# Three changes together in a fused attention and MLP kernel: a reordered prologue, a product copy moved from VectorE to ScalarE, and one partial sum moved to TensorE

## The reference

```
ada = silu(c) @ Wada.T + bada          # six vectors per batch: shift, scale, gate, twice
h = rmsnorm(x) * (1 + scale_msa) + shift_msa
q, k, v = split_heads(h @ Wqkv.T + bqkv)
q, k = rmsnorm(q) * hd**-0.5, rmsnorm(k)
o = softmax(q @ k.T) @ v
x = x + gate_msa * (o @ Wproj.T + bproj)
h = rmsnorm(x) * (1 + scale_mlp) + shift_mlp
x = x + gate_mlp * (gelu(h @ Wfc1.T + bfc1) @ Wfc2.T + bfc2)
```

## Time and profile before

| | us |
|---|---|
| median of 3 runs | 1811.17 |
| lowest, highest | 1810.55, 1813.67 |
| the profiled execution's own time | 1810.62 |
| its span in the trace | 1808.8 |
| L = 0 begins (first `qk`) | 68.8 |
| L = 64 begins | 343.8 |
| L = 208 begins | 848.2 |
| the MLP's first loop begins, about | 1000 |

### The profile page before, as it was taken

One profiled execution on the slowest core, in us unless ns is written; L12 is line 12 of the kernel. 1 busy time (PEld: TensorE's weight loads), 2 busy tenths in 40 slices (PEclk: granted clock), 3 DMA queues, 4 the chain that ended last, 5 costly groups with the idle time before them and its releaser, 6 DMA issues.

```text
span 1808.8 us, 23247 instructions
## 1 busy us (share of the span) xinstructions
PE 1727.9 (96%) x8376; PEld 1154.5 (64%) x8376; DVE 1085.6 (60%) x1325; ACT 919.6 (51%) x1136; POOL 372.5 (21%) x305
## 2 busy tenths in 40 slices
PE   6998999999999999999889999999999999999998
PEld 3554555555555555554224787878788887878786
DVE  6678888898898898878788545142332324142301
ACT  4476666777777777778787432222221212221221
POOL 3001111100001000000140233333332333333332
PEclk8999999999999999999999899999999999999999
DMA  5754545555555555555765201010020202010000
GB/s 195 214 144 132 135 123 139 132 147 135 154 135 134 146 130 156 127 135 153 174 144 196 74 18 58 25 52 24 12 70 6 64 17 64 17 52 23 17 18 24
DMA packets 122242, 176.92 MB, mean 98 GB/s; under 512 B 29568, under 2 KB 43904, under 8 KB 121136
## 3 DMA queue, kind: packets, MB, share of 16 engines
q1 hardware_dynamic: 115952, 156.41, 32.3%
q10 hardware_dynamic: 5408, 16.81, 2.5%
q0 software_dynamic: 800, 2.62, 0.5%
HBM read 124.87 MB, written 50.92 MB: 97 GB/s over the span
## 4 chain that ended last, share of the span: by engine, by line
PE 44%; issue 29%; DVE 11%; POOL 9%; ACT 4%; DMA 2%; SPq 0%; POOLq 0%; ACTq 0%; DVEq 0%
PE scores L513 9%; PE pv L530 8%; PE gemm L588 7%; DVE sums L791 5%; PE scores L1303 5%; POOL act_parts L1235 5%; PE gemm L601 4%; ACT probs L704 3%; PE pv L1320 3%; PE gemm L1320 2%; PE aux L554 2%; POOL y L1233 2%; PE aux L547 1%; DVE raw L816 1%; DVE raw L862 1%
## 5 line engine op out<-in xcount | busy, mean ns | idle before, releaser
L704 ACT ACTIVATE probs<-scores,shift 128x1024 f32<-128x1024 f32 x512 | 548.7, 1113 | 195.4 <-PE scores L513 178.7
L791 DVE TENSOR_TENSOR sums<-sums,probs 128x2048 f32<-128x2048 f32 x192 | 453.8, 2363 | 32.7 <-ACT probs L704 28.0
L513 PE MATMUL scores<-q_stack,k_stack 128*128 128x512 f32 x1024 | 358.8, 435 | 6.3 <-ACT probs L704 6.1
L1303 PE MATMUL scores<-w_hi,act_parts 128*128 128x512 f32 x1024 | 318.7, 392 | 0.0
L513 PEld LDWEIGHTS scores<-q_stack,k_stack 128*128 128x128 f32 x1024 | 173.8, 189 | 202.3 <-issue 105.5
L1235 POOL TENSOR_TENSOR act_parts<-act_full,act_parts 128x512 fp32r<-128x512 f32 x128 | 172.5, 1348 | 514.2 <-ACT act_parts L1166 513.6
L530 PE MATMUL pv<-probs,v 128*32 128x512 f32 x2048 | 253.1, 603 | 0.4 <-ACT probs L704 0.4
L1303 PEld LDWEIGHTS scores<-w_hi,act_parts 128*128 128x128 f32 x1024 | 191.4, 189 | 38.8
L1303 PE MATMUL scores<-w_lo,act_parts 128*128 128x512 f32 x512 | 199.9, 391 | 0.0
L1373 DVE TENSOR_TENSOR y_next<-pv,p_bias 128x512 f32<-128x512 f32 x28 | 19.3, 691 | 299.7 <-PE pv L1275 299.7
L1166 ACT ACTIVATE act_parts<-act_full 128x512 fp32r<-128x512 f32 x128 | 80.9, 632 | 224.5 <-PE scores L1303 223.5
(11 more groups left out here) (167 smaller groups left out, 1944.1 us busy)
## 6 DMA issues: line engine op xcount, KB each, us to landing
k_stack<-parts_scratch SPq DMA_DIRECT2D x128, 256.0 KB, 5.0
q_stack<-parts_scratch SPq DMA_DIRECT2D x128, 256.0 KB, 5.1
parts_scratch<-parts SPq DMA_DIRECT2D x62, 512.0 KB, 2.9
inverse<-inverse_scratch SPq DMA_DIRECT2D x128, 64.0 KB, 2.1
heads_out<-o_out SPq DMA_DIRECT2D x32, 256.0 KB, 5.2
out<-result SPq DMA_DIRECT2D x32, 256.0 KB, 2.0
heads<-heads_out SPq DMA_DIRECT2D x28, 256.0 KB, 3.6
x_tile<-in_x SPq DMA_DIRECT2D x28, 256.0 KB, 2.8
```

Source lines behind the costliest of these rows:

```text
L513: mm = nc.tensor.matmul(scores[p][:, i, :], k_stack[s][:, h, j * P:(j + 1) * P], q_stack[half][:, h, :], start=True, stop=True)
L704: nc.scalar.activation(probs[L % RING][:, 2 * p:2 * p + 2, :], scores[p][:], ACT.Exp, bias=small["shift"][:]).then_inc(exp_done, 1)
L791: nc.vector.tensor_tensor(sums[:], a[:], probs[l % RING][:], ALU.add).then_inc(added, 1)
L1303: mm = nc.tensor.matmul(acc[t], act_parts[m % 2][:, b, t * P:(t + 1) * P], w2[a][:, m, :], start=(m == 0 and i == 0), stop=(m == NM - 1 an ...
```

## The change

It has three parts, made together.

1. **Prologue.** The first products are now nine, in the order v, k, q, v, v, v, v, k, q; the sixth v tile moves behind L = 0, and the three v tiles of steps 0 to 2 take one step each. The tables of statistics, turns and weight splits are shifted. The four later blocks of `wadaT` are loaded by SyncE as soon as the third block of `wqkvT` has landed, ahead of `v_bias` and `qk_bias` in SyncE's order, in place of ScalarE's queue at L = -14.
2. **Units.** For L >= 0 `raw_out` runs on ScalarE, in the unit's last step behind the step's two exponentials, and `square` follows it at once; the sum of squares comes a step earlier. A third buffer for `raw` is taken from the x tiles, which go from three buffers to two. For batches 2 and 3 the turn of an x tile is a step later (odd steps in place of even ones). `make_parts` always follows the addition of its step in the main loop.
3. **Row sums.** For groups hh >= LEAN = 26 the eighth key tile isn't added by VectorE: TensorE adds it by four more matmuls with `ones` onto the row sums.

```diff
 NU = 2 * NH
 SEEN = HG * CH // P
 XS = 3
+XB = 2
 AFTER = B * BSTEPS
...
@@ -80,11 +81,10 @@
...
-START, AFTER_LAST = -25, 2
-PLAN = placed(-18, 0, [v_of(0, 1), v_of(1, 1), v_of(2, 1), k_of(0, 0, 1), q_of(0, 0, 1), v_of(3, 1), v_of(4, 1), v_of(5, 1),
-                       k_of(0, 1, 1), q_of(0, 1, 1)])
+START, AFTER_LAST = -27, 2
+PLAN = placed(-18, 0, [v_of(0, 1), k_of(0, 0, 1), q_of(0, 0, 1), v_of(1, 1), v_of(2, 1), v_of(3, 1), v_of(4, 1), k_of(0, 1, 1), q_of(0, 1, 1)])
 FIRST_PRODUCTS = len(PLAN)
-PLAN += placed(0, 0, [v_of(6, 1), v_of(7, 2), k_of(1, 0, 2), q_of(1, 0, 2), k_of(1, 1, 2), k_of(2, 0, 2), q_of(2, 0, 2),
+PLAN += placed(0, 0, [v_of(5, 1), v_of(6, 1), v_of(7, 1), k_of(1, 0, 2), q_of(1, 0, 2), k_of(1, 1, 2), k_of(2, 0, 2), q_of(2, 0, 2),
                       q_of(1, 1, 2), k_of(3, 0, 2), q_of(3, 0, 2), k_of(2, 1, 2), q_of(2, 1, 2), k_of(3, 1, 2), q_of(3, 1, 2)])
...
-STAT = [-24, -23, -22, -21, -20, -19, -18, -17]
-NORM = [-23, -22, -21, -20, -19, -18, -17, -16]
-TURN = [-24, -23, -22, -21, -19, -18, -17, -16] + [19, 21, 23, 27, 31, 35, 39, 45]
-HOUT = [-19, -19, -18, -18, -17, -16, -15, -15]
+STAT = [-26, -25, -24, -23, -22, -20, -18, -16]
+NORM = [-25, -24, -23, -22, -21, -19, -16, -15]
+TURN = [-25, -24, -23, -22, -18, -17, -16, -15] + [19, 21, 23, 27, 31, 35, 39, 45]
+HOUT = [-22, -20, -21, -19, -17, -15, -14, -13]
 for b in range(2, B):
-    TURN += [BSTEPS * b - 78 + 8 * t for t in range(NT)]
+    TURN += [BSTEPS * b - 77 + 8 * t for t in range(NT)]
 STAT += [step - 1 for step in TURN[NT:]]
 NORM += TURN[NT:]
 HOUT += [step + 1 for step in TURN[NT:]]
-SPLIT = [-19, -18, -17, -16, -15, -14, -13, -12] + [step + 1 for step in HOUT[NT:]]
+SPLIT = [-21, -20, -19, -18, -15, -14, -13, -12] + [step + 1 for step in HOUT[NT:]]
 STAT_AT, NORM_AT, TURN_AT, SPLIT_AT = ({step: n for n, step in enumerate(table)} for table in (STAT, NORM, TURN, SPLIT))
 HOUT_ACT = {step: n for n, step in enumerate(HOUT) if n < NT and n % 2 == 1}
 HOUT_AT = {step: n for n, step in enumerate(HOUT) if n not in HOUT_ACT.values()}
-XLOAD_AT = {step + 1: n + XS for n, step in enumerate(TURN) if NT <= n < B * NT - XS}
-XLOAD_AT.update({NT + n: NT + n for n in range(XS)})
-SPLIT_W = {"act": {-23: 0, -20: 1, -17: 2}, "dve": {-20: 0, -19: 1, -16: 2}}
-ROW_MM, ROW_MOVED, MOD_TURN, MOD_MADE, GAINS = {-25: 0, -24: 1}, {-24: 0, -22: 1}, -23, -20, -18
-ADA_LOAD, ADA_BIAS, ADA_MM, ADA_MADE, ADA_STORED = -14, -9, -8, -5, 2
-
-RAW_AT = {step + 1: n for n, step in enumerate(UNIT_END)}
+XLOAD_AT = {step + 1: n + XB for n, step in enumerate(TURN) if NT <= n < B * NT - XB}
+XLOAD_AT.update({NT + n: NT + n for n in range(XB)})
+SPLIT_W = {"act": {-24: 0, -20: 1, -18: 2}, "dve": {-22: 0, -20: 1, -19: 2}}
+ROW_MM, ROW_MOVED, MOD_TURN, MOD_MADE, GAINS = {-27: 0, -26: 1}, {-26: 0, -25: 1}, -25, -23, -18
+ADA_BIAS, ADA_MM, ADA_MADE, ADA_STORED = -9, -10, -5, 2
+RAW_AT = {step + (1 if step < 0 else 0): n for n, step in enumerate(UNIT_END)}
 SUM_AT = {}
 for n, step in enumerate(UNIT_END):
-    step += 1 if step < 0 else 2
+    step += 1
     while step in SUM_AT or step in ROWS_AT or step in TURN_AT and step >= 0:
         step += 1
     SUM_AT[step] = n
 INV_AT, FIN_AT = ({step + after: n for step, n in SUM_AT.items()} for after in (1, 2))
+LEAN = -(-max(FILL) // NT)
+def adds_until(l):
+    hh, j = l // NT, l % NT
+    return ADDS * min(hh, LEAN) + (ADDS - 1) * max(0, hh - LEAN) + (min(j, ADDS - 1) if hh >= LEAN else j)
...
     def x_of(n):
-        return xt[n % XS] if n < XS or n >= NT else mem["x_ahead"][n - XS]
+        return xt[n % XB] if n >= NT else xt[n] if n < XS else mem["x_ahead"][n - XS]
     x_ahead_in = [sem(f"x_ahead_in{n}") for n in range(NT)]
     def x_landed(n):
         if n < NT:
             return x_ahead_in[n], 16
-        return x_in[n % XS], 16 * sum(1 for m in range(NT, n + 1) if m % XS == n % XS)
+        return x_in[n % XB], 16 * ((n - NT) // XB + 1)
+    def raw_of(n):
+        return raw[n % 2] if n < 4 else (raw + [xt[XB]])[n % 3]
...
@@ -394,7 +407,7 @@
         def load_x(n):
             if n >= NT:
-                sp.wait_ge(turned, n - XS + 1)
+                sp.wait_ge(turned, n - XB + 1)
...
         setup["sync"](sp, load_x)
+        sp.wait_ge(setup["wqkv_in"][2], 16)
+        for i in range(NA_LATER):
+            cols = slice((NA_NOW + i) * CH, (NA_NOW + i + 1) * CH)
+            sp.dma_start(ada_w[i], dram["wadaT"][:, cols].rearrange("(k p) n -> p k n", p=P)).then_inc(ada_w_in[i], 16)
         sp.dma_start(v_bias[:], dram["bqkv"][2 * D:3 * D].rearrange("(a n) -> a n", a=1).broadcast_to([P, D])).then_inc(const_in, 16)
         sp.dma_start(qk_bias[:], dram["bqkT"]).then_inc(const_in, 16)
...
         def row_sums(hh):
-            pe.wait_ge(added, ADDS * (hh + 1))
+            pe.wait_ge(added, adds_until(NT * hh + NT - 1))
             aux_free()
             for h in range(HG):
-                mm = nc.tensor.matmul(aux[h * DH:(h + 1) * DH, :], small["ones"][:], sums[:, h, :], start=True, stop=True)
+                mm = nc.tensor.matmul(aux[h * DH:(h + 1) * DH, :], small["ones"][:], sums[:, h, :], start=True, stop=(hh < LEAN))
+            if hh >= LEAN:
+                l = NT * hh + NT - 1
+                pe.wait_ge(exp_done, 2 * l + 2)
+                for h in range(HG):
+                    mm = nc.tensor.matmul(aux[h * DH:(h + 1) * DH, :], small["ones"][:], probs[l % RING][:, h, :], start=False, stop=True)
             mm.then_inc(rs_mm, 1)
             issued["rows"] += 1
...
+        def raw_out(n):
+            b, g, which, half = UNIT[n]
+            col = (0 if which == "q" else NG) + g
+            act.wait_ge(unit_mm, n + 1)
+            act.wait_ge(part_lo, max(4, n - 2))
+            nc.scalar.activation(raw_of(n)[:], bank_of_product(PRODUCT_OF_UNIT[n])[:], ACT.Identity, bias=qk_bias[:, col:col + 1]).then_inc(raw_done, 1)
         def square(n):
             act.wait_ge(raw_done, n + 1)
             if n > 0:
                 act.wait_ge(ss_mm, n)
-            nc.scalar.activation(squares[:], raw[n % 2][:], ACT.Square).then_inc(sq_done, 1)
+            nc.scalar.activation(squares[:], raw_of(n)[:], ACT.Square).then_inc(sq_done, 1)
...
-                act.wait_ge(added, ADDS * (l // NT) + max(1, l % NT))
+                act.wait_ge(added, adds_until(l + 1 if l % NT == 0 else l))
+                if l // NT >= LEAN and l % NT == NT - 1:
+                    act.wait_ge(rs_mm, l // NT + 1)
...
-            if L == ADA_LOAD:
-                for i in range(NA_LATER):
-                    cols = slice((NA_NOW + i) * CH, (NA_NOW + i + 1) * CH)
-                    act.dma_start(ada_w[i], dram["wadaT"][:, cols].rearrange("(k p) n -> p k n", p=P)).then_inc(ada_w_in[i], 16)
...
             if L >= 0:
                 exponentials(L, 0)
                 exponentials(L, 1)
+            if L >= 0 and L in RAW_AT:
+                raw_out(RAW_AT[L])
+                square(RAW_AT[L])
             if L in ROWS_AT:
                 move_rows(ROWS_AT[L])
             if L in INV_AT:
                 inverse_root(INV_AT[L])
-            if L in RAW_AT:
+            if L < 0 and L in RAW_AT:
                 square(RAW_AT[L])
...
         def add(l):
             j, hh = l % NT, l // NT
-            if j == 0:
+            if j == 0 or hh >= LEAN and j == NT - 1:
                 return
             dve.wait_ge(exp_done, 2 * l + 2)
             if j == 1:
@@ -786,7 +818,7 @@
                     dve.wait_ge(rs_mm, hh)
                 a = probs[(l - 1) % RING]
             else:
-                dve.wait_ge(added, hh * ADDS + j - 1)
+                dve.wait_ge(added, adds_until(l - 1))
                 a = sums
...
         def make_parts(n):
-            r = raw[n % 2]
+            r = raw_of(n)
...
-            parts_first = L in FIN_AT and (L < 0 or L in RAW_AT and RAW_AT[L] == FIN_AT[L] + 2)
+            parts_first = L in FIN_AT and L < 0
             if parts_first:
                 make_parts(FIN_AT[L])
-            if L in RAW_AT:
+            if L < 0 and L in RAW_AT:
                 raw_out(RAW_AT[L])
```

More of the change, by code:

```diff
@@ L312, in build_setup @@
                 scalar_row=scalar_row, tensor_first=tensor_first, tensor_row=tensor_row, tensor_turn=tensor_turn, vector_first=vector_first, vector_x_gain=vector_x_gain,
-                vector_gains=vector_gains, vector_split=vector_split, vector_mod=vector_mod, low=low, mod_ready=mod_ready)
+                vector_gains=vector_gains, vector_split=vector_split, vector_mod=vector_mod, low=low, mod_ready=mod_ready, wqkv_in=wqkv_in)
 def build_attention(nc, sem, small, dram, mem, psum, mlp):
@@ L815, in raw_out @@
                 dve.wait_ge(part_lo, n - 1)
-            nc.vector.tensor_scalar(raw[n % 2][:], bank_of_product(PRODUCT_OF_UNIT[n])[:], qk_bias[:, col:col + 1], None, ALU.add).then_inc(raw_done, 1)
+            nc.vector.tensor_scalar(raw_of(n)[:], bank_of_product(PRODUCT_OF_UNIT[n])[:], qk_bias[:, col:col + 1], None, ALU.add).then_inc(raw_done, 1)
```

## The result

The changed kernel takes 1824.8 us (median of 4 runs, 1823.01 to 1826.67) where the kernel before, run beside it, takes 1812.42 (1810.55 to 1813.89): ratio 1.0068, 95% interval 1.005 to 1.0087. It is slower by 12.4 us; the forecast was 1807.0, in a range from 1798 to 1816. The profiled execution took 1823.01 us, its span is 1821.2.

A forecast was written before the change was run, and what follows sets the result against it. TensorE's own work was taken to set the time, so only idle gaps and half-clock stretches could change: 1810.6 + 4.0 - 11 + 8 - 5 = 1806.6, with the median's 0.5 us 1807.1, stated as 1807.0 us, range 1798 to 1816.

The forecast's parts named there:

- Units up to L = 63, -11 us: Crowded stage before L = 64: ScalarE's copies replace waits on VectorE's backlog and half clock goes; -11 us (-17 to -3).
- the first rival: Steps 16 to 56: ScalarE becomes the bound, gain shrinks to -2, time 1816; chance 0.22, shared with the fixed waits.
- Units from L = 64, +8 us (3 to 12): L = 64 to 207: ScalarE's copy can't start before the second exponential ends, and moved turns leave gaps; +8 us.
- Prologue, +4.0 us (-3 to +9): Before and just behind L = 0: biases land late behind four loads, sixth v tile moves; +4.0 us.
- the biases are in time: Prologue: loads share, L = 0 begins near 66, copy as cheap as the plain one; 1802 or 1799, chance 0.18.
- Row sums, -5 us (-8 to +1): End of the kernel: waits for VectorE's last addition shrink, clock returns, four more matmuls per group cost; -5 us.
- the parts cancel: Whole kernel: crowded-stage gains equal the later fixed waits, with a prologue at +7; 1811 us, chance 0.15.

The follow-up runs named there:

- units alone: Kernel before plus only ScalarE's copy and square, third raw buffer, two x buffers, sums one step behind, turns one step later: 1826.93 us, ratio 1.0095.
- run with undelayed biases: Kernel before plus only the new prologue order and moved v tile, the four later weight loads left on ScalarE: 1817.99 us, ratio 1.0037.
- row sums alone: Kernel before plus only TensorE adding the eighth key tile for groups 26 to 31: 1802.64 us, ratio 0.9963.

## Why the prediction was wrong

**The step that failed is "Units up to L = 63, -11 us".** From L = 8 to L = 64 the units gave -1.7 us at equal clock (240.3 against 241.9), and in steps 0 to 7 they cost +2.0: in sum about nothing, outside the term's bounds of -17 to -3. In the changed kernel TensorE's waits in this stage come to 17.6 us where the term left 12.4 of the old 16.9: 6.4 for ScalarE's copies (7.6 with steps 0 to 7; I had 8), 3.7 for exponentials (2.4), 4.1 for v tiles (2) and 3.4 for a turn (nothing). These are 5.2 us more, and the 5.5 us of clock did not come back. So the price of the late copies was near enough, and what the term had wrong is that VectorE would be in time once the copies were gone.
- I took VectorE's backlog for an effect of the copies. It is one of VectorE's whole load, above all the additions, and taking 17 us of copies off it left it late: halving the additions too brought the stage from 240.3 to 226.2 us, of which 3.4 is clock. The gaps changed their cause, as the first rival had it. Its number for this term (-2) was nearly right, its culprit not: the trace has no wait of ScalarE for a raw buffer here, and ScalarE is busy for 179 of 243 us; it waits for VectorE.
- The 5.5 us of clock were to come back with the gaps of over 2 us (of the four gaps before, two were 1.9 to 2.0). A gap of 3.4 us stayed, one of 1.8, and half clock also began at 313.4 us, behind gaps of 1.1 and 0.9 alone; the changed kernel lost the same 6.8 us.
- I priced the place of the sums as a part of ScalarE's copy (ten even ends at 0.8 us, and 0.6 at four logarithms); no line asks what it would be worth to leave it. In steps 0 to 63, 9 of 23 sums stand at odd steps, where it was 2; their even ends lose the work that would have filled the gap and get a logarithm ahead of their exponentials. With the sums two steps behind, as before, the stage takes 5.1 us less, steps 0 to 7 1.8 less and the stage from L = 64 on 2.9 less. So the unit part with the sums left in their place gave -6.7 us in this stage at equal clock, with 11.7 us of waits for VectorE's v tiles and normalisations left.

**Units from L = 64, +8 us (3 to 12)**: +10.9 (+11.2 in the units alone). TensorE's waits for the copy are the ones that I had put there (over 12 us):

```profile
PE gemm L611 <- ACT raw L699: 7.6, 9, 0.8
PE gemm L611 <- ACT xt L699: 4.2, 5, 0.8
PE gemm L624 <- ACT raw L699: 2.5, 3, 0.8
```

The turns' share was too high (5.0 forecast, 2.1 measured) and the sums' distance, 2.9, was missing. The copy took 0.69 us, where I had assumed 0.70:

```profile
L699 ACT ACTIVATE raw<-gemm,qk_bias 128x512 f32<-128x512 f32 x40 | 27.5, 688 | 0.0
```

That is within 0.02 us of 0.706 us, the estimate for 512 columns by the formula with a tile bias in the Trainium skill, "ScalarE: Activation LUTs", section "What ACT_TABLE_LOAD costs".

But that a late copy is a fixed price was too simple: with sums and turns where they fill the gap, the regular groups cost no more than before.

**Prologue, +4.0 us (-3 to +9)**: +5.0, by other ways. The biases landed 3 us earlier than forecast (39.0, not 42), and it didn't matter: the run with undelayed biases has its first copy no earlier. So L = 0 moved by 0.1 to 0.6 us instead of 0.9, but the stretch behind it by 4.5 instead of 3.1, of which 1.9 was four additions on VectorE ahead of a copy, which I hadn't looked for. The 4 KB of `qk_bias` took 9.7 us behind the four loads. This agrees with the rule in the Trainium skill, "DMA: Bandwidth & Descriptors", section "Queues, rings and completion order", that each DMA engine takes the descriptors of one ring in order; that it goes round between two rings, no run here shows for the biases. The rival that the biases are in time and L = 0 begins near 66 found no support: with biases at 26.0 the first copy came no earlier.

**Row sums, -5 us (-8 to +1)**: -8.2 by the medians, with an interval of -9.4 to -3.8 that holds the -5 too. The profiled stage fell by 7.5 us: all 7.3 us of waits went, and 3.4 us of clock, while the added matmuls of four groups took 4.2 us (1.05 each, where I had 0.87). I had taken the clock's loss from one execution; other kernels with the old row sums lost up to 6.8 there, and that goes too.

**Steps 208 to 248** in the units alone took 5.8 us more, which I forecast as nothing; with the row-sum part 1.3 is left (103.7 against 102.3), and the changed kernel has one gap of 1.6 us there, for which the profile names no wait, that the row sums alone don't have.

**The rival "the parts cancel"** (1811) has a slip in its sum: a prologue at +7 and row sums at -5, with the units cancelling, give 1812.6, or 1813 by the median.

## What to carry to other kernels

Before an operation is moved off a late engine, halve that engine's largest other work for one run. It shows what the lateness costs in all (here 12 us of the stage at equal clock), and so whether the move is large enough: 17 us of copies off a load of 203 left the engine late, and the gaps stayed under other names. A schedule's distances (here, how many steps a reduction follows its product) decide which engine's gap is filled and what stands ahead of the critical exponentials; a shift by one step was worth 15 to 18 us, more than the 6.7 us that the rest of the unit part gave in the stage with the wait, so move one thing at a time, and only in the stage where the trace shows the wait. Of a change in three parts, time each by itself: here one was worth 7 to 8 us and was hidden by the others.

## What the runs showed of the hardware

- The normalisation of a 128x512 tile on VectorE took 1.48 us at 172.65 us, where 0.55 us is usual; GpSimd split h (1.27 us, 128x512) at the same time. In the same way an addition of 2.28 us took 3.20. In the traces before and after, each addition of 128x2048 that took over 2.45 us ran beside a GpSimd instruction. That the one slows the other is argued from this alone; no run took GpSimd away.
- The half clock ahead of L = 0 took 5.1, 6.8 or 8.5 us in kernels with the same schedule up to there, so a single profile can't tell a few us.
- A gap of TensorE does not settle its clock: behind 2.92 us in step 1 of the changed kernel it stayed full, and at 313.4 us it was halved behind gaps of 1.14 and 0.85 us.
- The biased 128x512 copy from PSUM took ScalarE 0.69 us and VectorE 0.75 us.
